# Four layers of graph network on one core: the features loaded first, and a second projection in three 16-bit passes, its unit's parts at other distances

## The reference, cut to what matters

```python
h = relu(ln(x));  x = x + adj @ (h @ W0 + b0) / colsum(adj)[:, None]              # layer 0
h = relu(ln(x));  A = adj + I;  d = rowsum(A) ** -0.5
                  x = x + relu((A * d[:, None] * d[None, :]) @ (h @ W1))           # layer 1
h = relu(ln(x));  v = h @ W2;  n = v / max(norm(v), 1e-8)
                  x = x + softmax(n @ n.T + log(adj + 1e-8)) @ v + bias            # layer 2
h = relu(ln(x));  inc = adj + (adj > 0) / norm(rows)
                  x = x + (inc @ h) / rowsum(inc)                                  # layer 3
```

## Time and profile before

| what | value |
|---|---|
| median of three executions | 1412.53 us (1409.02 to 1413.61) |
| the profiled execution: its own time | 1413.93 us |
| its span | 1412.1 us |
| TensorE busy | 1354.4 us, 96% of the span |
| VectorE busy | 835.5 us, 59% |
| ScalarE busy | 531.0 us, 38% |
| GpSimd busy | 122.9 us, 9% |
| TensorE waiting for VectorE's low half (L610), first stage | 16.7 us in 8 waits |
| TensorE waiting for VectorE's normalized rows (L794), second stage | 7.4 us in 28 waits |
| mean granted clock of TensorE | 0.993 |

### The profile page before, as it was taken

The page is one execution under the profiler, slowest core; times in us unless marked ns, Lnnn a source line. Parts: engine busy times, 40 slices in busy tenths (PEclk is TensorE's granted clock), DMA queues, the critical chain, the costliest instruction groups (busy, mean ns, idle before and its releaser), DMA issues.

```text
span 1412.1 us, 26260 instructions
## 1 busy us (share of the span) xinstructions
PE 1354.4 (96%) x10186; PEld 1024.9 (73%) x10186; DVE 835.5 (59%) x1741; ACT 531.0 (38%) x1239; POOL 122.9 (9%) x193
## 2 busy tenths in 40 slices
PE   2899999989999999999999999999999999999999
PEld 1688888864455555567777777777777777888887
DVE  4789998858334443367667767767777877000000
ACT  2477645626222222244444544544545544000000
POOL 1100000012322222220000000000000000000000
PEclk8899999999999999999999999999999999999999
DMA  9998999610111110100001000001001003222221
GB/s 223 251 323 295 395 401 390 253 64 16 54 51 60 45 61 16 45 24 31 31 31 39 31 31 24 31 32 38 31 24 33 29 24 118 83 83 90 83 84 31
DMA packets 52746, 141.16 MB, mean 100 GB/s; under 512 B 7568, under 2 KB 16784, under 8 KB 52624
## 3 DMA queue, kind: packets, MB, share of 16 engines
q1 hardware_dynamic: 50224, 137.39, 29.8%
q10 hardware_dynamic: 2400, 2.10, 0.4%
HBM read 118.49 MB, written 20.97 MB: 99 GB/s over the span
## 4 chain that ended last, share of the span: by engine, by line
PE 82%; DVE 10%; SPq 2%; ACT 2%; issue 2%; POOL 1%; DMA 1%; DVEq 0%; ACTq 0%; POOLq 0%
PE ps L1291 15%; PE ps L1292 15%; PE ps L1305 11%; PE ps L1158 7%; PE ps L1159 7%; PE ps L1196 5%; PE ps L1197 5%; PE ps L1322 4%; PE ps L1341 4%; PE ps L1353 4%; PE ps L1252 2%; DVE ring L606 1%; SPq L299 1%; DMA acc<-in_adj 1%; POOL small L512 1%
## 5 line engine op out<-in xcount | busy, mean ns | idle before, releaser
L1158 PE MATMUL ps<-val_hi,ring 128*128 128x257 f16 x1024 | 226.2, 273 | 0.0
L1159 PE MATMUL ps<-val_lo,ring 128*128 128x256 f16 x1024 | 226.2, 273 | 0.0
L1292 PE MATMUL ps<-acc,ring 128*128 128x256 f16 x1024 | 225.8, 273 | 0.0
L1291 PE MATMUL ps<-acc,ring 128*128 128x256 f16 x1024 | 225.8, 271 | 0.0
L1196 PE MATMUL ps<-ring,acc 128*128 128x512 fp8e4 x512 | 194.9, 381 | 4.0 <-DVE acc L740 3.9
L1305 PE MATMUL ps<-hnt 128*128 128x512 f16 (+3 forms) x864 | 196.3, 363 | 0.0
L1197 PE MATMUL ps<-ring,acc 128*128 128x512 fp8e4 x512 | 194.8, 380 | 0.0
L1103 ACT ACTIVATE ring<-ring 128x512 f16<-128x512 f32 (+2 forms) x133 | 79.3, 596 | 227.7 <-DVE ring L864 227.4
L606 DVE STREAM_TRANSPOSE ring<-acc 128x1024 uint8<-128x1024 uint8 x128 | 151.3, 1217 | 21.5 <-DMA acc<-in_adj 21.3
L864 DVE SCALAR_TENSOR_TENSOR ring<-ring,ps 128x512 f32<-128x512 fp8e4 (+2 forms) x133 | 85.7, 645 | 119.2 <-PE ps L1341 119.2
L1291 PE MATMUL ps<-val_hi,hs 128*128 128x257 f16 x534 | 145.8, 273 | 0.6 <-DVE hs L845 0.6
(11 more groups left out here) (150 smaller groups left out, 2060.4 us busy)
## 6 DMA issues: line engine op xcount, KB each, us to landing
acc<-in_adj SPq DMA_DIRECT2D x256, 256.0 KB, 7.1
ring<-at_dram SPq DMA_DIRECT2D x56, 512.0 KB, 3.9
at_dram<-ring SPq DMA_DIRECT2D x32, 512.0 KB, 8.7
ring<-at_dram SPq DMA_DIRECT2D x64, 256.0 KB, 2.8
xs<-in_x SPq DMA_DIRECT2D x16, 256.0 KB, 12.8
out<-xs ACTq DMA_DIRECT2D x14, 128.0 KB, 3.8
out<-xs SPq DMA_DIRECT2D x14, 128.0 KB, 3.0
w_all<-in_L_gnn_weight SPq DMA_DIRECT2D x2, 256.0 KB, 13.8
```

Of the source, the lines that this page charges most:

```text
L1158: nc.tensor.matmul(ps[:, k % 8, 0:D + 1], lhs, val_hi0[:, t, 0:D + 1], start=(t == 0), stop=False)
L1159: last = nc.tensor.matmul(ps[:, k % 8, 0:D], lhs, val_lo0[:, t, :], start=False, stop=(t == NB - 1))
L1291: nc.tensor.matmul(ps[:, bank, 0:n], lhs, hi[:, t, 0:n], start=start, stop=False)
L1292: return nc.tensor.matmul(ps[:, bank, 0:D], lhs, lo[:, t, :], start=False, stop=stop)
```

## The change

Three things are changed.

**Loads and the scale.** The first four tiles of x are now the first loads, with a semaphore of their own (`x_first`); W0, b0 and tiles 4 to 7 follow. VectorE does the statistics of tiles 0 to 3 first and the maxima after them. `partition_all_reduce` is gone for W0: VectorE spreads the partition's maximum along a 128 x 128 tile (`wide`), TensorE multiplies it by the identity, which turns partitions into columns, and VectorE reduces the result from PSUM. GpSimd does one power at once, on constants. The `partition_all_reduce` for W1 and W2 stays.

**First stage.** Quarters of adjacency are taken at another pace: one in two steps up to step 7, then one per step, so that step `s` takes quarter `s - 4` (`quarters_by`). Block `b` opens for pieces at step `4b + 9`. The column sums move to steps 24 and 30 on VectorE, and start at step 21 instead of 17 on ScalarE.

**Second projection.** W2 is split into high and low halves (`w2_hi` on ScalarE at `h == 28`, `w2_lo` on VectorE at `k == 16`), the rows `ht` too: ScalarE writes the high half and VectorE the low half (`rows_low`, new). `project2` is then three 16-bit passes, six matmuls, in place of 32 bits, and waits for `rows_low`. The parts of a unit lie at 4, 7 and 10 steps in place of 3, 5 and 8. On VectorE `normalize2` now precedes `hnt_low(i - 1)`. Waits for `ht2_ready` on TensorE become waits for `ht2_low`.

```diff
+        w2_hi = w_all[:, 512:768].bitcast(F16).rearrange("p (c d) -> p c d", c=C)
+        w2_lo = w_all[:, 768:1024].bitcast(F16).rearrange("p (c d) -> p c d", c=C)
...
+        wide = y0[:, 1, 0:P]
...
+        def quarters_by(s):
+
+            return s // 2 if s < 8 else s - 4
...
-                    open_b = [b for b in range(GB) if s >= 4 * b + 5 and progress[b] < min(NB, s - 4)]
+                    open_b = [b for b in range(GB) if s >= 4 * b + 9 and progress[b] < min(NB, s - 4)]
...
-            return ht[i % 2] if i < FIRST_LATE else ht_late[i % 2]
+            rows = (ht[i % 2] if i < FIRST_LATE else ht_late[i % 2]).bitcast(F16)
+            return rows[:, 0:D], rows[:, D:2 * D]
...
+            for a in (0, 2, 1, 3):
+                sp.dma_start(xs[32 * a:32 * a + 32, 0:GB, :], x_q[a, :, 0:GB, :]).then_inc(sem["x_first"], 16)
             sp.dma_start(w[:, 0, :, :], wv[0]).then_inc(sem["w_loaded"], 16)
             sp.dma_start(bias_bc, b0.partition_broadcast(P)).then_inc(sem["b_loaded"], 16)
-            load_x(sp, 0, (0, 2, 1, 3))
+            for a in (0, 2, 1, 3):
+                sp.dma_start(xs[32 * a:32 * a + 32, GB:8, :], x_q[a, :, GB:8, :]).then_inc(x_loaded[0], 16)
...
-            pool.wait_ge(sem["wmax_part"], 2)
-            pool.partition_all_reduce(wmax[:, 0:2], wpart[:, 0:2], P, RMAX).then_inc(sem["wmax_all"], 1)
+            pool.memset(one, 1.0).then_inc(sem["one_set"], 1)
             pool.wait_ge(sem["half_set"], 1)
+            pool.wait_ge(sem["one_set"], 1)
+            nc.gpsimd.tensor_tensor(f3[:, 0:GB], one, half[:, 0:GB], ALU.pow).then_inc(sem["power_set"], 1)
...
-            dve.wait_ge(sem["w_loaded"], 16)
-            nc.vector.tensor_reduce(wpart[:, 0:1], w[:, 0, :, :], AX.XY, ALU.max,
-                                    apply_absolute_value=True).then_inc(sem["wmax_part"], 1)
-            dve.wait_ge(sem["b_loaded"], 16)
-            nc.vector.tensor_reduce(wpart[:, 1:2], bias_bc, AX.X, ALU.max,
-                                    apply_absolute_value=True).then_inc(sem["wmax_part"], 1)
...
-                if t % 8 == 0:
+                if t == 0:
+                    dve.wait_ge(sem["x_first"], 64)
+                elif t == GB or t % 8 == 0:
                     dve.wait_ge(x_loaded[t // 8], 64)
...
 
             for t in range(GB):
                 stats0(t)
-
-            dve.wait_ge(sem["wmax_all"], 1)
-            nc.vector.tensor_tensor(p2[:, 0:1], wmax[:, 0:1], wmax[:, 1:2], ALU.max).then_inc(sem["p2_clamped"], 1)
+            dve.wait_ge(sem["w_loaded"], 16)
+            nc.vector.tensor_reduce(wpart[:, 0:1], w[:, 0, :, :], AX.XY, ALU.max,
+                                    apply_absolute_value=True).then_inc(sem["wmax_part"], 1)
+            dve.wait_ge(sem["b_loaded"], 16)
+            nc.vector.tensor_reduce(wpart[:, 1:2], bias_bc, AX.X, ALU.max,
+                                    apply_absolute_value=True).then_inc(sem["wmax_part"], 1)
+            dve.wait_ge(sem["wmax_part"], 2)
+            nc.vector.tensor_tensor(wmax[:, 0:1], wpart[:, 0:1], wpart[:, 1:2], ALU.max).then_inc(sem["p2_clamped"], 1)
             dve.wait_ge(sem["p2_clamped"], 1)
+            dve.wait_ge(sem["ident_f"], 1)
+            nc.vector.tensor_scalar(wide, ident_f[:, :], 0.0, wmax[:, 0:1], ALU.mult, ALU.add).then_inc(sem["wide_ready"], 1)
+            shift0(0)
+            stats0(GB)
+            dve.wait_ge(sem["spread"], 1)
+            nc.vector.tensor_reduce(p2[:, 0:1], ps[:, 3, 0:P], AX.X, ALU.max).then_inc(sem["wmax0_ready"], 1)
+            dve.wait_ge(sem["wmax0_ready"], 1)
             nc.vector.tensor_scalar(p2[:, 0:1], p2[:, 0:1], 2.0 ** -60, None, ALU.max).then_inc(sem["p2_clamped"], 1)
             dve.wait_ge(sem["p2_clamped"], 2)
             nc.vector.tensor_scalar(p2[:, 0:1].bitcast(I32), p2[:, 0:1].bitcast(I32), EXPONENT_BITS, None,
                                     ALU.bitwise_and).then_inc(sem["p2_masked"], 1)
             dve.wait_ge(sem["p2_masked"], 1)
             nc.vector.reciprocal(p2i[:, 0:1], p2[:, 0:1]).then_inc(sem["p2_inv"], 1)
-            shift0(0)
             dve.wait_ge(sem["p2_inv"], 1)
             nc.vector.tensor_scalar(wsc, p2i[:, 0:1], VSC, None, ALU.mult).then_inc(sem["wsc_ready"], 1)
-            for t in range(GB, AHEAD0):
+            for t in range(GB + 1, AHEAD0):
                 stats0(t)
             dve.wait_ge(sem["wsc_ready"], 1)
...
             for s in range(STEPS0):
                 if s + AHEAD0 < NB:
                     stats0(s + AHEAD0)
-                if s < NB:
-                    transposed(s // 4, s % 4)
+                for n in range(quarters_by(s), quarters_by(s + 1)):
+                    transposed(n // 4, n % 4)
                 if s % GB == 2 and s // GB + 1 < NG:
                     shift0(s // GB + 1)
                 if 3 <= s < NB + 3:
                     low0(s - 3)
-                if s in (22, 28):
-                    column_sums(0, (s - 22) // 6, GW)
+                if s in (24, 30):
+                    column_sums(0, (s - 24) // 6, GW)
...
+                if k == 16:
+                    dve.wait_ge(sem["w2_high"], 1)
+                    nc.vector.tensor_tensor(w2_lo, w[:, 2, :, :], w2_hi, ALU.subtract).then_inc(sem["w2_low"], 1)
...
                 nc.vector.tensor_scalar(xn[u], xs[:, k, :], mv[u][:, 0:1], rstd[u],
...
+            def rows_low(i):
+
+                dve.wait_ge(sem["ht2_ready"], i + 1)
+                nc.vector.scalar_tensor_tensor(ht_of(i)[1], ps[:, bank_t(i), 0:D], 0.0, ht_of(i)[0],
+                                               ALU.max, ALU.subtract).then_inc(sem["ht2_low"], 1)
...
                 residual2(i)
+                normalize2(i)
                 if i > 0:
                     hnt_low(i - 1)
-                normalize2(i)
+                rows_low(i)
                 values2(i)
                 unit_rows(i)
...
+                if n in late_at["transposes2"]:
+                    rows_low(late_at["transposes2"][n])
...
-                if 17 <= s < 33:
-                    column_sum(0, 8 + s - 17, GW)
-                if s >= 33:
-                    column_sum(0, 24 + 2 * (s - 33), GW)
-                    column_sum(0, 25 + 2 * (s - 33), GW)
+                if s >= 21:
+                    column_sum(0, 8 + s - 21, GW)
+            for t in range(24, NB):
+                column_sum(0, t, GW)
...
+                if h == 28:
+                    act.wait_ge(sem["w1_low"], 1)
+                    nc.scalar.activation(w2_hi, w[:, 2, :, :], ACT.Copy).then_inc(sem["w2_high"], 1)
...
-                nc.scalar.activation(ht_of(i), ps[:, bank_t(i), 0:D], ACT.Relu).then_inc(sem["ht2_ready"], 1)
+                nc.scalar.activation(ht_of(i)[0], ps[:, bank_t(i), 0:D], ACT.Relu).then_inc(sem["ht2_ready"], 1)
...
+            pe.wait_ge(sem["wide_ready"], 1)
+            nc.tensor.matmul(ps[:, 3, 0:P], wide, ident_f[:, :], start=True, stop=True).then_inc(sem["spread"], 1)
...
-                    for kind, done in (("project1", "relu1"), ("transposes2", "ht2_ready"),
+                    for kind, done in (("project1", "relu1"), ("transposes2", "ht2_low"),
...
                 pe.wait_ge(sem["xn2_ready"], i + 1)
-                since(pe, sem["ht2_ready"], i)
+                since(pe, sem["ht2_low"], i)
...
             def project2(i, n=None):
-                pe.wait_ge(sem["ht2_ready"], i + 1)
+                pe.wait_ge(sem["ht2_low"], i + 1)
+                pe.wait_ge(sem["w2_low"], 1)
                 since(pe, sem["sumsq_ready"], i)
                 bank_free(n)
                 for c in range(C):
-                    last = nc.tensor.matmul(ps[:, bank_2(i), 0:D], ht_of(i)[:, c * P:(c + 1) * P], w[:, 2, c, :],
-                                            start=(c == 0), stop=(c == C - 1))
+                    high, low = (rows[:, c * P:(c + 1) * P] for rows in ht_of(i))
+                    nc.tensor.matmul(ps[:, bank_2(i), 0:D], high, w2_hi[:, c, :], start=(c == 0), stop=False)
+                    nc.tensor.matmul(ps[:, bank_2(i), 0:D], high, w2_lo[:, c, :], start=False, stop=False)
+                    last = nc.tensor.matmul(ps[:, bank_2(i), 0:D], low, w2_hi[:, c, :], start=False, stop=(c == C - 1))
                 last.then_inc(sem["o2_done"], 1)
...
                 for i in range(FIRST_LATE):
                     if T == starts[i]:
                         project1(i)
-                    if T == starts[i] + 8:
+                    if T == starts[i] + 10:
                         transposes_n(i)
-                    if T == starts[i] + 3:
+                    if T == starts[i] + 4:
                         transposes2(i)
-                    if T == starts[i] + 5:
+                    if T == min(starts[i] + 7, NT1 - 1):
                         project2(i)
```

7 lines of the change are left out of this document (3 added, 4 removed).

## The result

| | before | after |
|---|---|---|
| median of 20 executions each | 1413.03 us (1409.02 to 1415.19) | 1416.53 us (1412.61 to 1421.2) |
| ratio, 95% interval | | 1.0027 [1.0018, 1.0036] |
| the profiled execution: its own time, span | 1413.93, 1412.1 us | 1421.2, 1419.4 us |
| TensorE waiting for the normalized rows, second stage | 7.4 us in 28 waits | 19.3 us in 26 waits |

The account below looks back on a forecast made before the run. TensorE's work and waits were taken to set the pace almost everywhere, loads up to about 48 us. Start -6.0 and second stage +7.3 gave +1.3 us: 1415.2 profiled, 1414 us on the median's level, range 1406 to 1421.

Parts of the forecast that it names:

- rival 2: Start gives less than 3 us because later halves' loads wait, second-stage units cost in full: 1419 us, chance 0.22.
- The start, -6.0: First stage: slower taking of quarters has more work done when the fifth half lands; 6.0 us earlier, bounds 0 to 7.5.
- Rival 3: Second stage: list order binds, but short units and groups cost half; -6.5 + 2.5 = -4, 1408 us, chance 0.16.
- E + 4.74: Second stage: the next unit's transposes can't start before 4.74 us after E, the end of project2 on TensorE.
- the interval of 8.26: Second stage, normal unit, transposes to transposes: 3.52 us to project2's end plus 4.74; before it was 8.38.
- the short units: Units 1, 8, 15 and 22, six steps after the one before: intervals of 8.92 us, four times, 35.7 us.
- the groups: Units 5, 10, 14 and 19, with z_low between: intervals of 9.54 us, four times, 38.2 us.
- Rival 1: Second stage: new distances take the waits away, no wait in a unit; 1391 us, chance 0.08.
- Unit 24 at 11.5: Second stage: unit 24 can't begin before its group is out; interval 11.5 us, project1 idle about 3.5 us.
- The identity's additions: GpSimd, five times in the second stage: bound of 0.5 us more per chain, not in the sum.
- Late units, +0.4: After the second stage's units: rows_low delays transposes by 0.3 and mirror by 0.9, four projections return 0.85; +0.4 us.
- the last, -0.2: Last unit of the second stage: its lighter 16-bit projection, 0.66 instead of 0.87 us, gives -0.2 us.

Follow-up runs that it names:

- e5: The kernel after, unchanged, timed again on another chip: 1419.25 us, beside 1414.34 for the kernel before (ratio 1.0036).
- e8: The kernel after with the old pace of adjacency quarters, pieces and column sums; x first and the TensorE maximum stay: 1425.09 us, 1.0073 of before.
- e3: The kernel after with second-stage distances 4, 6 and 9 instead of 4, 7 and 10: 1396.22 us, 0.9886 of before.
- e4: The kernel after with VectorE's unit_rows moved behind the next unit's residual2, distances kept: 1403.53 us, 0.9931 of before.
- e6: The kernel after with the old distances 3, 5 and 8, 16-bit passes kept: 1400.99 us, 0.9903 of before.
- e7: The kernel after with the second projection in four 32-bit passes, distances 4, 7 and 10 kept: 1421.81 us, 1.0047 of before.
- e9: The kernel after with 30 unused matmuls filling TensorE's idle time ahead of unit 24: 1414.37 us, 1.0004 of before.
- e2: The kernel before with only the new second projection and its distances 4, 7 and 10: 1425.08 us, 1.0092 of before.
- e12: The kernel after with distances 4, 6 and 9, identity additions and groups moved, VectorE's unit_rows order as in after: 1387.47 us, 0.9810 of before.
- e11: The kernel after with distances 4, 6 and 9, unit_rows behind the next residual, identity additions and groups moved: 1403.17 us, 0.9923 of before.

## Why the prediction was right

Its mechanism held, and so did its sum of two large opposite terms, to 2.2 us: +3.5 by the medians, +1.3 in the forecast. The time alone would not have told it from rival 2, for 1416.5 lies as near to 1419 as to 1414; the traces do. And the profiled execution, for which the forecast gave 1415.2, took 1421.2, six more: three terms that stood at nothing, below, all went the same way, and in the median they weigh less. Step by step:

- *The start, -6.0.* Right in the main: 5.8 in the first pair of traces; with the landing of the load taken out 4.9 there and 6.1 by e5 and e8, and e8 gives 5.8 in time. The 1.2 between the two lies ahead of the change of stages (259.4 us from the landing to it in after, 258.2 in e5) and fits the wait of 1.10 us for the sixth half. So what rival 2 feared seems to have happened, in a small part and not each time. That loads and scale cost nothing, and that the first row's 8 us give nothing, fits e8. Timed alone it is 4.5 [2.8, 6.5]. The working has a slip: 298.0 - 27 x 7.02 is 108.5 and not 108.6, so the stretch took 58.7 us with 4.5 of waits, and the sum gives -5.8. (Rival 3's sum takes the start at -6.5, for which no row is given.)
- *E + 4.74 and the interval of 8.26.* Exact, as are 8.92 at the short units; 9.46 at the groups where 9.54 was worked out. e3, e4, e6 and e7 move it as it says. Rival 1 (no waits) is excluded by 26 waits, rival 3 (special units at half cost) by 8.92 and 9.46, rival 2 (the start gives less than 3 us) by the saves and by e8.
- *Unit 24 at 11.5.* Right as a chain: 11.52 in e8 and e9. Mis-sized as a time: 14.38 in the profile, since the clock fell behind 3.5 us of idle time. The forecast named the idle time and priced the wait alone, though the trace of before had the fall behind 3.34 us. +2.9 where it fell fully.
- *The identity's additions.* These stood as a bound ("0.5 more, five times") and in the sum as nothing. They cost 0.36 five times, +1.8, and by another way: VectorE's instructions are slower beside them.
- *Late units, +0.4, and the last, -0.2.* Right where the clock stays up (814.1 against 813.9 from unit 27 to the end). In after, e2, e5, e6 and e12 it is 815.6 to 815.7: the clock falls again there for some 3 us, behind waits of 1.5 and 0.9 us. In e3, e4 and e8 to e11, with the same two waits (1.42 to 1.53, and 0.94), it does not.

The sum by the profiles: 370.85 to 365.34 is -5.5, unit 0 to 27 +11.0, the rest +1.8: +7.3, the difference of the spans. Without the two falls of the clock it is -5.5 + 8.2 + 0.1 = +2.8. The medians, +3.5 and +4.9, lie between; that not every execution has both falls would explain it, and the two groups of granted clocks under e9 speak for it, but only one execution of each run has a trace.

## What to carry to other kernels

Room given to each part of a pipelined unit is not room for the unit: in an engine's list the last instruction of one unit stands ahead of the first of the next, so count from the end of the latest part of unit i to the first product of unit i+1, along the lists. Here two steps more ahead of the second projection cost 18 us (e6 against e5), and one step fewer gave back about as much (e3 is 16.2 us under before, after 3.5 and 4.9 above it, on different chips). When a wait of some microseconds stands ahead of TensorE, price also what follows it: behind waits of 2.64 to 3.50 us the clock was at half for 3 to 7 us in most profiles here. And a single profile of a start that loads rule can be off by up to 4 us: subtract the landing time before comparing.
